# Grouped attention: the scores of two query tiles issued together, the turning four tiles behind, and the other products in two blocks per unit

## What is computed

```python
h = _rms(x, ln_w)
q = (h @ wq).reshape(B, S, NHEADS, HEAD_DIM)      # 32 heads of 64
k = (h @ wk).reshape(B, S, KVHEADS, HEAD_DIM)     # 8 heads of 64
v = (h @ wv).reshape(B, S, KVHEADS, HEAD_DIM)
q, k = _rope(q, k)
k = jnp.repeat(k, g, axis=2); v = jnp.repeat(v, g, axis=2)
scores = jnp.einsum('bqhd,bkhd->bhqk', q, k) / np.float32(np.sqrt(HEAD_DIM))
scores = jnp.where(causal[None, None], scores, jnp.float32(-1e+30))
attn = jax.nn.softmax(scores, -1)
o = jnp.einsum('bhqk,bkhd->bqhd', attn, v).reshape(B, S, NHEADS * HEAD_DIM)
x = x + o @ wo
```

## Time and profile before

| | |
|---|---|
| Median of 3 runs | 2865.11 us (2864.5 to 2866.74) |
| Profiled execution, its own time | 2874.59 us |
| Its span, first to last instruction | 2872.4 us |
| PE busy over the span | 2343.5 us (82%) |
| DVE, ACT, POOL busy | 1704.7 (59%), 1284.7 (45%), 1312.5 us (46%) |
| Mean granted TensorE clock | 0.908 of full speed |

### The profile page before, as it was taken

How to read it: one execution, slowest core, us unless ns; L and a number is a source line. 1 busy time by engine, 2 the same in 40 slices (tenths; PEclk the granted TensorE clock), 3 DMA queues, 4 the chain that set the end, 5 groups by cost and what they waited for, 6 DMA issues and landing times. The chain is left out here.

```text
span 2872.4 us, 42222 instructions
## 1 busy us (share of the span) xinstructions
PE 2343.5 (82%) x12088; PEld 1564.5 (54%) x12088; DVE 1704.7 (59%) x5428; ACT 1284.7 (45%) x3719; POOL 1312.5 (46%) x1245
## 2 busy tenths in 40 slices
PE   6999999974999999999994999714856657599992
PEld 5888888862555555555553665412322323467661
DVE  7666776656767767767763433276565646553334
ACT  3444444433666666566663444312544435243331
POOL 3444444432555555556551588623021220128885
PEclk9999999996999999999996899956969687699996
DMA  5000000011000000000006355420000000425554
GB/s 162 16 15 15 15 5 10 15 37 52 1 1 1 1 1 1 1 1 1 1 1 240 61 85 87 80 70 0 1 0 0 0 0 0 149 64 86 86 86 112
DMA packets 72548, 112.05 MB, mean 39 GB/s; under 512 B 11505, under 2 KB 59377, under 8 KB 71985
## 3 DMA queue, kind: packets, MB, share of 16 engines
q0 software_dynamic: 30336, 42.73, 9.2%
q1 hardware_dynamic: 37824, 63.15, 6.3%
q10 hardware_dynamic: 4224, 4.19, 0.4%
HBM read 80.69 MB, written 36.32 MB: 41 GB/s over the span
## 5 line engine op out<-in xcount | busy, mean ns | idle before, releaser
L1059 POOL TENSOR_TENSOR b_sm<-b_sm,b_rden 128x128 f32<-128x128 f32 (+3 forms) x512 | 355.6, 722 | 357.4 <-DVE b_rden L1012 357.4
L952 ACT ACTIVATE b_sm<-b_sm,b_mn 128x128 f32<-128x128 f32 (+3 forms) x512 | 285.0, 569 | 22.9 <-DVE b_mn L1004 22.0
L943 ACT ACTIVATE b_pt<-b_t 128x128 f32<-128x128 f32 (+3 forms) x512 | 196.0, 439 | 144.9 <-PE b_t L883 144.5
L1004 DVE CUSTOM_DVE_ANT_0 b_sm<-b_f,maskB 128x128 f32<-128x128 f32 (+3 forms) x512 | 233.5, 489 | 3.3 <-issue 2.2
L873 PE MATMUL b_f<-b_k,b_q 64*128 64x128 f32 (+3 forms) x1024 | 209.9, 486 | 29.1 <-DVE b_prod L993 14.7
L993 DVE SCALAR_TENSOR_TENSOR b_prod<-b_f,b_sin 32x512 f32<-32x512 f32 x320 | 219.8, 687 | 4.3
L1428 POOL DMA_INDIRECT XN<-rows,m_slots x158 | 158.2, 1001 | 94.0 <-issue 47.2
L883 PE MATMUL b_t<-ident,b_sm 128*128 128x128 f32 x1280 | 194.6, 283 | 0.9 <-ACT b_pt L943 0.8
L883 PEld LDWEIGHTS b_t<-ident,b_sm 128*128 128x128 f32 x1280 | 143.4, 141 | 87.3 <-issue 60.5
L409 POOL TENSOR_TENSOR a_q<-a_prod 128x512 f32<-128x512 f32 x64 | 81.8, 1278 | 228.5 <-DVE a_prod L355 228.5
L2010 DVE TENSOR_REDUCE c_nm<-c_first 128x2 f32<-128x1024 f32 x128 | 149.8, 1219 | 35.2 <-PE c_first L1801 35.2
(11 more groups left out here) (277 smaller groups left out, 5442.7 us busy)
## 6 DMA issues: line engine op xcount, KB each, us to landing
WM<-in_m_w_dram SPq DMA_DIRECT2D x4, 3072.0 KB, 17.3
WM<-in_m_w_dram SPq DMA_DIRECT2D x4, 2432.0 KB, 14.2
acc<-in_zeros_dram SPq DMA_DIRECT2D x3, 2176.0 KB, 15.9
n_part<-acc SPq DMA_DIRECT2D x12, 512.0 KB, 7.1
a_wa<-in_a_wa_dram SPq DMA_DIRECT2D x8, 512.0 KB, 4.7
b_w<-in_b_w_dram SPq DMA_DIRECT2D x1, 3072.0 KB, 10.0
XN<-rows,m_slots POOLq DMA_INDIRECT x158
X<-in_x_dram SPq DMA_DIRECT2D x4, 512.0 KB, 5.6
```

The source lines that it names most:

```text
L943: act.activation(pt[:, M % 2, head, 0:t + 1, t * P:(t + 1) * P], back_bank(("t", S, head))[:, 0:keys(t)].rearrange("p (k n) -> p k n", n=P ...
L952: act.activation(sm[:, s, 0:keys(t)], sm[:, s, 0:keys(t)], ACT.Exp, scale=-1.0, bias=mn[:, s:s + 1], accum_out=den[:, s:s + 1]).then_inc(s ...
L1004: dve.tensor_tensor_reduce(sm[:, s, 0:keys(t)], front_bank(("s", S, head))[:, 0:keys(t)], mask[:, SEQ - keys(t):SEQ], 1.0, -3 * NEG, ALU.a ...
L1059: pool.tensor_tensor(sm[:, s, 0:keys(t)], sm[:, s, 0:keys(t)], rden[:, s:s + 1].to_broadcast([P, keys(t)]), ALU.mult).then_inc(s_pn, 1)
```

## The change

The loops of TensorE and the two bank lists now go over S in steps of two. The scores of the steps S and S+1 are issued together, so that all four `front` banks are filled in a row. LAG becomes 4. The rest of a unit stands in two blocks:

- after the scores of j=0 and j=1: turning of S-4 (128 keys), the query projection, turning of S-3 (384 keys), first half of `out_proj`;
- after the scores of j=2 and j=3: `values`, turning of S-4 (256 keys), the projection of `beside`, second half of `out_proj`, turning of S-3 (512 keys).

On the other engines `copy_out` moves ahead of `copy_pt` and `exp` at j=2, `copy_v` to j=3 behind `exp`, `rotate` of the queries from j=0 to j=1 and of the keys from j=1 to j=3, and the two `add`s one and two steps later. The banks, the buffers and the ring of 12 rows keep their sizes, and no instruction is added or removed.

```diff
--- before.py
+++ after.py
@@ -748,7 +748,7 @@
     TOTAL = UNITS * STEPS_OF
     LAST = (UNITS + 3) * STEPS_OF
     RING = 12
-    LAG = 3
+    LAG = 4
 
 
     def beside(M):
@@ -762,18 +762,18 @@
 
     HEAD = [("v", 0, t) for t in range(TB)] + [("k", 0, 0), ("q", 0, 0), ("q", 1, 0)]
     fronts, backs = list(HEAD), []
-    for S in range(LAST):
+    for S in range(0, LAST, 2):
         M, j = S // STEPS_OF, S % STEPS_OF
         if S < TOTAL:
-            fronts += [("s", S, 0), ("s", S, 1)]
+            fronts += [("s", S + n // 2, n % 2) for n in range(4)]
         if j == 0 and M + 2 < UNITS:
             fronts.append(("q", M + 2, 0))
-        if j == 1 and beside(M) is not None:
+        if j == 2 and beside(M) is not None:
             fronts.append(beside(M))
+        if j == 2 and 0 <= M - 2 < UNITS:
+            backs.append(("o", M - 2, 0))
         if 0 <= S - LAG < TOTAL:
-            backs += [("t", S - LAG, 0), ("t", S - LAG, 1)]
-        if j == 0 and 0 <= M - 2 < UNITS:
-            backs.append(("o", M - 2, 0))
+            backs += [("t", S - LAG + n // 2, n % 2) for n in range(4)]
     FRONT = {use: at for at, use in enumerate(fronts)}
     BACK = {use: at for at, use in enumerate(backs)}
     JOBS = {job: at for at, job in enumerate(use for use in fronts if use[0] != "s")}
@@ -914,23 +914,26 @@
                 pe.wait_ge(s_w, 16 * 5)
                 for job in HEAD:
                     project(job)
-                for S in range(LAST):
+                for S in range(0, LAST, 2):
                     M, j = S // STEPS_OF, S % STEPS_OF
                     turns, ends = 0 <= S - LAG < TOTAL, 0 <= M - 3 < UNITS
                     if S < TOTAL:
                         scores(S)
-                    if j == 1 and beside(M) is not None:
-                        project(beside(M))
-                    if j == 1 and ends:
-                        out_proj(M - 3, 0)
+                        scores(S + 1)
+                    if j == 2 and 0 <= M - 2 < UNITS:
+                        values(M - 2)
                     if turns:
                         transposes(S - LAG)
                     if j == 0 and M + 2 < UNITS:
                         project(("q", M + 2, 0))
-                    if j == 0 and 0 <= M - 2 < UNITS:
-                        values(M - 2)
-                    if j == 3 and ends:
+                    if j == 2 and beside(M) is not None:
+                        project(beside(M))
+                    if j == 2 and ends:
                         out_proj(M - 3, 1)
+                    if turns:
+                        transposes(S - LAG + 1)
+                    if j == 0 and ends:
+                        out_proj(M - 3, 0)
 
             @block.scalar
             def _(act):
@@ -969,13 +972,13 @@
                     copy_v(job)
                 for S in range(LAST):
                     M, j = S // STEPS_OF, S % STEPS_OF
+                    if j == 2 and 0 <= M - 2 < UNITS:
+                        copy_out(M - 2)
                     if 0 <= S - LAG < TOTAL:
                         copy_pt(S - LAG)
                     if S < TOTAL:
                         exp(S)
-                    if j == 0 and 0 <= M - 2 < UNITS:
-                        copy_out(M - 2)
-                    if j == 1 and beside(M) is not None and beside(M)[0] == "v":
+                    if j == 3 and beside(M) is not None and beside(M)[0] == "v":
                         copy_v(beside(M))
 
             @block.vector
@@ -1029,9 +1032,9 @@
                         inverse(S - 1)
                     if j == 0 and M > 3 and M % B_UNITS == 3:
                         add_y(M // B_UNITS - 1)
-                    if j == 0 and M + 2 < UNITS:
+                    if j == 1 and M + 2 < UNITS:
                         rotate(("q", M + 2, 0))
-                    if j == 1 and beside(M) is not None and beside(M)[0] == "k":
+                    if j == 3 and beside(M) is not None and beside(M)[0] == "k":
                         rotate(beside(M))
                 add_y(BATCH - 1)
 
@@ -1065,10 +1068,10 @@
                     M, j = S // STEPS_OF, S % STEPS_OF
                     if S >= 1:
                         normalise(S - 1)
-                    if j == 1 and M + 2 < UNITS:
+                    if j == 2 and M + 2 < UNITS:
                         add(("q", M + 2, 0))
-                    if j == 2 and beside(M) is not None and beside(M)[0] == "k":
-                        add(beside(M))
+                    if j == 0 and M > 0 and beside(M - 1) is not None and beside(M - 1)[0] == "k":
+                        add(beside(M - 1))
 
 
 TOP_K = 4
```

## The result

The changed kernel takes 3036.65 us (median of 4 runs, 3033.52 to 3040.63) against 2865.93 before: ratio 1.0588, 95% interval 1.0559 to 1.0617. Slower, by 171 us. Its profiled execution took 3033.52 us, with a span of 3031.6, against 2874.59 and 2872.4 before.

The account below looks back on a forecast made before the run. TensorE's own instruction stream was taken to bound the stage. Added unit time of 148 us plus 30 us for the clock made 178, taking the median from 2865.1 to 3043 us, range 2990 to 3105.

Parts of the forecast that it names:

- What bounds the kernel: Inside the stage TensorE's own instruction stream is the time, short of that by 0.7 us in 27 units.
- What it takes away: Per unit, five changes of array shape instead of nine: 0.8 us less TensorE work, 51 us over 64 units.
- The rival built on it: Bank waits are hidden and four changes of array shape decide: 51 us won, 2814 us; chance 0.04.
- The query projection in the ring: j=3 scores can't start sooner than 5.56 us after the projection; only 3.81 lie between, at least 1.75 new waiting.
- key units: Units with a key projection: the 5.56 us applies a second time, 16.66 against 14.05 us, +2.6.
- The loop through ScalarE: In units without `beside`, copies, `exp`, `inverse`, `minimum` and `rotate` hold the next scores: 13.48 against 11.54 us, +1.95.
- the VectorE side: At `rotate` in units without `beside`, VectorE's queue is later than the ready query projection, deciding by 0.3 us.
- value units: Units with a value projection: `copy_v` is behind `exp` of j=3, 17.36 against 13.97 us, +3.4.
- The sum: Added time over the stage's units: 35 x 1.95 + 15 x 2.6 + 12 x 3.4 = 148 us.
- The clock: In the stage, falls to 1.2 GHz after new TensorE waits, 1.7 us each in 18 of 47: 30 us.
- Own time and median: Profiled execution goes to about 3053 us; its 9.5 us above the median carries over, so the median is 3043.

Follow-up runs that it names:

- the short `rotate`: Rotation's four instructions over 32 partitions made one over 128, no exchange of halves: kernel before 2835.16 us, changed kernel 2870.47 us.
- LAG 4: Kernel before with LAG 4 in place of 3, nothing else changed: 2878.28 us, ratio 1.0027.
- the spaced kernel: Changed kernel with `values` ahead of the second block, projection of `beside` straight behind the scores, its readers forward: 2829.95 us, ratio 0.9853.
- the late inverse: Changed kernel, VectorE order only: `inverse` of j=3 behind the next `minimum` of j=1, queries' `rotate` ahead of `inverse` of j=0: 3016.12 us.
- `values` ahead: Changed kernel with only `values` and `copy_out` moved ahead of the j=2 and j=3 scores: 2885.17 us, ratio 1.0042.
- the kernel with the moved turning: On top of the late inverse, the 256-key turning moved behind the projection of `beside` and second half of `out_proj`: 3101.69 us.

## Why the prediction was right

**What bounds the kernel.** Right: TensorE's stream with a ring of four banks. On the kernel before, inside the stage, the short `rotate` and LAG 4 both moved only the units that the ring touches.

**What it takes away.** 0.8 us per unit was reckoned from the earlier trace rows, 0.74 measured in the spaced kernel (11.54 to 10.80). The rows of the changed kernel show the loss at a single change: `out_proj` takes 0.86 us to the next start ahead of a turning (1130.66 to 1131.52) and 0.96 ahead of scores (1136.21 to 1137.17). The Trainium skill ("TensorEngine Tiling (Array Packing)", Key Properties) states that a change of tiling mode drains TensorE. The trace agrees with it, at 0.74 us for four changes. That the time is lost by a drain, and not in another way at the same places, no run here shows. The rival built on it lost because `rotate` gives the bank back after 5.56 us and not 3.8.

**The query projection in the ring.** Measured 5.56 us from projection to scores, to the hundredth, in key units. The distance that is left in the changed kernel, 1137.17 + 0.53 - 1133.84 = 3.86, was reckoned as 3.81.

**The loop through ScalarE.** Followed from the scores at 1126.19, the steps came at (in us after it): second head of the turning 4.22 (4.15 reckoned), `minimum` of j=1 8.60 (8.60), `rotate` 9.74 (9.84), next scores 13.36 (13.48). Key units 16.71 (16.66), value units 17.48 (17.36). I said that the VectorE side decides by 0.3; it is 0.17.

**The sum.** The terms 68 + 39 + 41 = 148 are for 62 units. 59 of them lie between first and last `values` and came to 60 + 37 + 42 = 139; the other three (two without `beside`, one key unit) lie at the start of the stage, which came out 8 us longer where they stand for 6.5. So 148 was reckoned and 147 measured. One thing was missing from the sum: the addition in three units, which waits for nothing but pushes `minimum` back in the loop. It was put at nothing and cost 3 us by itself, and with the stretches at 1.2 GHz that begin in its waits some 12. The other way, the time outside the stage was 9 us shorter, which nothing here explains.

**The clock** is the term that was mis-sized: 18 of 47 waits, 30 us, were forecast, nine low stretches and 19 us measured. Since three of the nine last 6.8 us, that is 2.1 us for each, and 1.6 for each 3.4 us, where 1.7 was reckoned. The price was right and the count too high: the ring waits were shorter in idle time than I took them, 1.5 to 1.7 us and not 2.0. And the three places where the clock fell every time, the additions, were not in the forecast. The count can't be had from the length of a wait alone: the wait of 2.29 us for `copy_v` is followed by a low stretch in one of the twelve value units of the changed kernel, in two of twelve with the late inverse, in seven with the short `rotate`, and in nine with `values` ahead. What sets them apart stays open.

**Own time and median.** The profiled execution took 3033.5 for 3053 forecast, and the median 3036.65 for 3043. That the profiled one would again be 9.5 above the median was wrong: it was 3 below. Part of the nearness of the median is this luck: the profiled execution became 159 us longer where 178 were forecast (147 for 148, 3 for none, 19 for 30, and 9 less outside the stage), and two thirds of this miss do not show in the median. The stage itself came 168.7 longer.

## What to carry to other kernels

Count the distance, in time, from a use of a ring bank to the use that needs it back, and compare it with how long the reader takes from the producer's start; issuing two groups together shortens that distance even if no work is added. Where both can be had, keep the grouping and put the longest product that needs no bank of that ring into the gap. When a product is moved, follow the chain of each reader behind it in its own engine's queue, not only of the one that the move is for: one turning moved behind two other products cost 85 us. And look for the rare jobs in each queue: an addition that comes three times in 64 units made the longest waits here.

## What was not expected of the hardware

A wait can be worth more than its length. Behind 2.3 to 3.4 us of TensorE idleness in one piece the following stretch was often granted 0.50, and the products in it took up to twice as long. In the kernel with the moved turning this made 2.6 of the 4.5 us that a key unit lost (16.7 to 21.2; the wait itself grew by 1.85). But the same 2.29 us wait had this effect in one unit of twelve in one kernel and in nine of twelve in another, and waits of 1.5 to 1.7 us, in nearly all units of the changed kernel, had it in a few. The three waits of 2.76 us had it every time. What else decides, these runs do not show.
